# GpSimd's deviations in two sets, its semaphore clears behind them, at the start of four stages

## What is computed

```python
h = K(log_dt, inv_A_real, A_imag, B_ri, x)            # state-space kernel as tokens, (8, 256, 256)
h = concat([cls_tok, h], axis=1)                      # 257 rows for each batch
h = h + banded_attention(layernorm(h))                # softmax of banded scores, projection
h = h + experts(layernorm(h))                         # top 2 of 8 experts, silu(xW1) * xW3, then W2
h = h + fused_attention_block(layernorm(h))           # 16 heads + sparse top-k branch, x = LN(src + fused),
                                                      # LN(x + relu(x ff1) ff2)
h = h + fp4_ffn(layernorm(h))                         # block-wise FP4 rounding of activations and weights

def layernorm(x):
    return (x - mean(x)) / sqrt(var(x) + 1e-5)
```

## Time and profile before

| what | value |
| --- | --- |
| median of 3 runs | 1482.91 us (1480.83 to 1487.86) |
| the profiled execution, its own time | 1477.99 us |
| its span, first to last instruction | 1476.2 us |
| mean granted TensorE clock | 0.832 of full |
| TensorE matmul, busy | 1118.4 us (76%) |
| VectorE, busy | 765.7 us (52%) |
| GpSimd, busy | 452.8 us (31%) |
| ScalarE, busy | 384.5 us (26%) |
| starts of the four stages in the span | about 281, 603, 1135 and 1282 us |

### The profile page before, as it was taken

One profiled execution on the slowest core, in us unless ns is written; L12 is line 12 of the kernel. 1 busy time (PEld: TensorE's weight loads), 2 busy tenths in 40 slices (PEclk: granted clock), 3 DMA queues, 4 the chain that ended last, 5 costly groups with the idle time before them and its releaser, 6 DMA issues. The chain is left out here.

```text
span 1476.2 us, 21690 instructions
## 1 busy us (share of the span) xinstructions
PE 1118.4 (76%) x6799; PEld 807.9 (55%) x6799; DVE 765.7 (52%) x1788; ACT 384.5 (26%) x951; POOL 452.8 (31%) x527
## 2 busy tenths in 40 slices
PE   0358886750999990359999999999734999779888
PEld 0257774650677660235665665665422899646555
DVE  8955663230122224445556556656512377578885
ACT  0333331000222220114333334333210444222221
POOL 5941010117000007511202202211000577456665
PEclk9989998555899995667779769878657899989999
DMA  6016000102121113144314315414031200000000
GB/s 217 2 41 216 0 0 1 54 15 100 55 64 58 60 48 99 36 77 95 85 34 105 84 32 105 96 37 90 18 74 37 101 0 0 1 1 14 14 7 22
DMA packets 53403, 81.06 MB, mean 55 GB/s; under 512 B 8544, under 2 KB 45736, under 8 KB 52176
## 3 DMA queue, kind: packets, MB, share of 16 engines
q1 hardware_dynamic: 50128, 71.71, 19.1%
q0 software_dynamic: 3200, 8.43, 1.8%
HBM read 52.23 MB, written 27.62 MB: 54 GB/s over the span
## 5 line engine op out<-in xcount | busy, mean ns | idle before, releaser
L1933 DVE TENSOR_REDUCE fa_nm<-fa_ps 128x2 f32<-128x514 f32 x128 | 82.9, 690 | 74.4 <-PE fa_ps L2154 73.6
L1292 PE MATMUL ex_ps<-we_raw,ex_xT 128*128 x320 | 118.3, 494 | 0.0
L1773 ACT ACTIVATE fa_eT<-fa_ps 128x512 f32<-128x512 f32 x128 | 73.6, 590 | 81.7 <-PE fa_ps L2207 80.3
L1086 POOL DMA_INDIRECT ex_got<-y_rows,ex_pos_i x34 | 32.1, 943 | 196.9 <-DMA y_rows<-ex_y 186.8
L2945 PE MATMUL qf_ps<-qf_wg,qf_xT 128*128 128x352 f32 x272 | 89.9, 480 | 2.1 <-ACT qf_xT L2786 1.4
L2154 PE MATMUL fa_ps<-fa_ks,fa_qs 64*128 64x258 f32 x256 | 71.4, 408 | 15.4 <-DMA fa_ks<-fa_qk_rows 10.8
L447 PE MATMUL tk_ps<-tk_u,tk_qb 64*32 64x64 f32 x1024 | 22.8, 266 | 71.4 <-POOLq L314 59.7
L2207 PE MATMUL fa_ps<-fa_qs,fa_ks 66*128 66x256 f32 x256 | 71.3, 373 | 6.9 <-ACT fa_eT L1773 6.9
L1219 DVE COPY ex_hT<-ex_ps 128x384 f32<-128x384 f32 x40 | 22.3, 558 | 100.1 <-PE ex_ps L1301 100.1
L2154 PEld LDWEIGHTS fa_ps<-fa_ks,fa_qs 64*128 64x128 f32 x256 | 50.7, 258 | 40.6 <-issue 23.4
L2945 PEld LDWEIGHTS qf_ps<-qf_wg,qf_xT 128*128 128x128 f32 x272 | 50.6, 194 | 37.3 <-issue 6.6
(11 more groups left out here) (435 smaller groups left out, 2509.3 us busy)
## 6 DMA issues: line engine op xcount, KB each, us to landing
we_raw<-in_L_ffn_W SPq DMA_DIRECT2D x24, 384.0 KB
fa_qs<-fa_qk_rows SPq DMA_DIRECT2D x16, 514.0 KB
fa_ks<-fa_qk_rows SPq DMA_DIRECT2D x32, 257.0 KB, 9.9
x_rows<-tk_zero SPq DMA_DIRECT2D x1, 5120.0 KB, 19.1
ex_xin<-x_rows SPq DMA_DIRECT2D x40, 128.0 KB
y_rows<-ex_y SPq DMA_DIRECT2D x40, 128.0 KB, 1.7
fa_rsb<-fa_rs_rows SPq DMA_DIRECT2D x8, 528.0 KB
fa_qk_rows<-fa_qhl SPq DMA_DIRECT2D x32, 128.5 KB
```

Of the source, the lines that this page charges most:

```text
L1086: g.indirect_dma_start(out=got[0:n, a, t, :], out_offset=None, in_=y_rows[:, :], in_offset=bass.IndirectOffsetOnAxis(ap=pos_i[0:n, a, t:t ...
L1292: last = mm(ps[:, bank + t % 2, 0:HD], xT[:, t % 2, k, :], raw[:, ds(e, 1), m, k * HD:(k + 1) * HD], start=(k == 0), stop=(k == KC - 1))
L1773: cp(eT[:, j % 8, :], ps[:, ST + j % 2, :], ACT.Exp).then_inc(z["e_ready"], 1)
L1933: nc.vector.tensor_reduce(nm[:, :, j], ps[:, b:b + 2, 0:TOK], AX.X, ALU.max, negate=True).then_inc(z["max_done"], 1)
```

## The change

In the experts, the feed-forward and the quantised part, GpSimd makes the deviations (and where there is one, the shift) of tiles 0 and 1 first, increments `norm_ready`, makes those of the other 15 tiles, increments it again, and only then clears the old semaphores. In the experts VectorE waits for the second increment after it has normalised tiles 0 and 1. In the feed-forward and the quantised part ScalarE waits for it after it has centred tiles 0 and 1. In the fused attention, whose deviations were in two sets already, the clears move from the start to behind the scaling of `wf_o`, ahead of the second set. In the feed-forward SP issues the columns first, with a semaphore of their own (`columns_in`) for which ScalarE waits, then W1 and W2, then the five rows, then the raw weights; `own_in` now counts the five rows, and GpSimd and VectorE wait for these.

```diff
--- before.py
+++ after.py
@@ -1052,10 +1052,12 @@
 
         @block.gpsimd
         def _(pool):
+            s = Steps(pool, z["pst"])
+            reciprocal_deviation(nc, pool, mem, s, (slice(0, 2),))
+            pool.sem_inc(z["norm_ready"], 1)
+            reciprocal_deviation(nc, pool, mem, s, (slice(2, TILES),))
+            pool.sem_inc(z["norm_ready"], 1)
             clear_spent(pool, mem)
-            s = Steps(pool, z["pst"])
-            reciprocal_deviation(nc, pool, mem, s)
-            pool.sem_inc(z["norm_ready"], 1)
             g = nc.gpsimd
 
             s(g.memset(ones[:, :], 1.0))
@@ -1135,6 +1137,8 @@
             for u in range(BATCH):
                 normalise(nc, mem, 2 * u, xn[:, 2 * u, :])
                 normalise(nc, mem, 2 * u + 1, xn[:, 2 * u + 1, :]).then_inc(z["xn_ready"], 1)
+                if u == 0:
+                    dve.wait_ge(z["norm_ready"], 2)
             normalise(nc, mem, CLS, xn[:, CLS, :]).then_inc(z["xn_ready"], 1)
 
             dve.wait_ge(z["lg_ps"], BATCH + 1)
@@ -1578,7 +1582,6 @@
 
         @block.gpsimd
         def _(pool):
-            clear_spent(pool, mem)
             s = Steps(pool, z["pst"])
             g = nc.gpsimd
 
@@ -1595,6 +1598,7 @@
             pool.wait_ge(z["sig_ready"], 1)
             step(g.tensor_scalar(w["o"][:, :, :], w["o"][:, :, :], sg[:, 0:1], None, ALU.mult))
             pool.sem_inc(z["wo_ready"], 1)
+            clear_spent(pool, mem)
             reciprocal_deviation(nc, pool, mem, s, (slice(2, CLS),))
             shift(nc, pool, mem, s, (slice(2, CLS),))
             pool.sem_inc(z["norm_ready"], 1)
@@ -2382,7 +2386,7 @@
     XB, HB, YB = 0, 2, 6
 
     names = ("norm_ready", "xn_ready", "x_ps", "xt_ready", "xb_ready", "hid_ps", "hid_ready", "y_ps", "ag_ready",
-             "dev_ready", "hb_ready", "h_done", "vst", "pst", "y_read", "fetched", "own_in", "f1_in", "f2_in", "w_scaled", "w_rounded", "dve_go", "pool_go")
+             "dev_ready", "hb_ready", "h_done", "vst", "pst", "y_read", "fetched", "own_in", "columns_in", "f1_in", "f2_in", "w_scaled", "w_rounded", "dve_go", "pool_go")
     z = {n: sem("ff_" + n) for n in names}
 
     def tile_of(t, u):
@@ -2400,10 +2404,11 @@
     with nc.Block() as block:
         @block.sync
         def _(sp):
-            for dst, src in own:
-                sp.dma_start(dst, src).then_inc(z["own_in"], 16)
+            sp.dma_start(*own[-1]).then_inc(z["columns_in"], 16)
             for name, (dst, src) in zip(("f1_in", "f2_in"), weights):
                 sp.dma_start(dst, src).then_inc(z[name], 16)
+            for dst, src in own[:-1]:
+                sp.dma_start(dst, src).then_inc(z["own_in"], 16)
             for dst, src in loads:
                 sp.dma_start(dst, src).then_inc(z["fetched"], 16)
             if loads:
@@ -2411,12 +2416,13 @@
 
         @block.gpsimd
         def _(pool):
+            s = Steps(pool, z["pst"])
+            for some in (slice(0, 2), slice(2, TILES)):
+                reciprocal_deviation(nc, pool, mem, s, (some,))
+                shift(nc, pool, mem, s, (some,))
+                pool.sem_inc(z["norm_ready"], 1)
             clear_spent(pool, mem)
-            s = Steps(pool, z["pst"])
-            reciprocal_deviation(nc, pool, mem, s)
-            shift(nc, pool, mem, s)
-            pool.sem_inc(z["norm_ready"], 1)
-            pool.wait_ge(z["own_in"], 16 * len(own))
+            pool.wait_ge(z["own_in"], 16 * len(own) - 16)
             s(nc.gpsimd.tensor_tensor(w["c2"][:, :], w["c2"][:, :], w["b1"][:, :], ALU.add))
             s.wait()
 
@@ -2496,7 +2502,8 @@
             act.wait_ge(z["norm_ready"], 1)
             centred(0, 0)
             centred(1, 1)
-            act.wait_ge(z["own_in"], 16 * len(own))
+            act.wait_ge(z["norm_ready"], 2)
+            act.wait_ge(z["columns_in"], 16)
             turned(0, 0)
             turned(1, 1)
             hidden(0, 0)
@@ -2548,7 +2555,7 @@
                 sums(u, p)
                 if not first:
                     finish(u - 1, 1 - p)
-            dve.wait_ge(z["own_in"], 16 * len(own))
+            dve.wait_ge(z["own_in"], 16 * len(own) - 16)
             s.begin()
             pipelined(dve, TILES, body)
             s.base, s.n = s.before + 6 * TILES - 3 + SCALED * PARTS, 0
```

## The result

| | before | after |
| --- | --- | --- |
| median | 1485.38 us (1480.83 to 1489.14, 4 runs) | 1464.85 us (1462.55 to 1468.01, 4 runs) |
| ratio, 95% interval | | 0.9882 (0.9847 to 0.9916) |
| profiled execution, span | 1477.99, 1476.2 us | 1462.55, 1460.8 us |
| mean granted TensorE clock | 0.832 | 0.842 |

The changed kernel is 1.2% faster; forecast were 1469.6 us and a range of 1464 to 1477. Timed twice more against the kernel before it gave ratios of 0.9921 (0.9893 to 0.9949) and 0.9909 (0.9884 to 0.9933), 11.7 and 13.5 us of some 1483, less than the 20.5 us between the medians of the first comparison.

What follows compares the result with a forecast made beforehand. A serial chain at each stage start (clears, deviations, centring, turning) was taken to bound what the edit can give. Savings 3.0 + 3.4 + 5.95 + 1.0 = 13.35 us give a median of 1469.6 us, range 1464 to 1477.

Steps and rivals of the forecast that it cites:

- The price of a clear: At the four stage starts: GpSimd's late first instruction is its semaphore clears, 66 to 72 ns each, 71 ns used.
- D: Rival, stage starts: delays are entry costs and stay, so only the split acts; 1483.7 us; chance 0.03.
- Experts: Experts' start: first gate products at 287.3 instead of 290.28, saving 3.0 us, or 2.3 by the port rule.
- port rule: Experts: VectorE's two normalises hold the port pair GpSimd needs, so the second set starts up to 0.7 us later.
- Fused attention: Fused attention's start: 54 clears leave the head, 3.9 us, less 0.45 us, saves 3.4 us; bounds 2.9 to 3.9.
- the collision: Fused attention: GpSimd, free only at 618.8, starts the low parts late after VectorE's high parts; SP passes on 0.45 us.
- rival B: Fused attention's loop: its phase eats the gain, seven units of 55.5 us against 53.5 cost 14 us; 1483.6; chance 0.06.
- C: Rival, fused attention's loop: granted clock falls, 9.4 us per TensorE-bound unit, 1507.4 us at four; slower; chance 0.04.
- Feed-forward: Feed-forward's start: turned(0) 6.7 us earlier, less 0.75 us for late bias rows, saves 5.95 us; bounds nothing to 6.4.
- A: Rival, feed-forward: rows land late, near 1154, with the 2.2 MB; only 7.4 us saved, 1475.5 us; chance 0.07.
- the late end: Feed-forward: W1 landing as late as 1143.95 against a need at 1142.1, which would cost 1.8 us.
- Quantised part: Quantised part's start: ScalarE copies turned weights from 1288.6 instead of 1289.63, handed on to the first grid; saves 1.0 us.

Runs made afterwards that it cites:

- waits moved: Changed kernel with four tiles in the experts' first set, second waits later, attention and feed-forward clears later, rows ahead of W2: 1465.95 us, ratio 0.9898 to the kernel before.
- best parts: The kernel with later second waits, but the experts' set whole and TensorE's wait for W2 moved to its first read: 1465.72 us, ratio 0.9876 to the kernel before.

## Why the prediction was right, and where it was not

**The price of a clear** holds: 66 to 72 ns before, 71 to 77 where they are doubled. The step that carries the forecast is confirmed by moving the clears and by doubling them, and D is excluded.

**Experts.** Forecast 3.0, measured 3.20, 3.45 and 3.02 less against the first profile of before. The trace differs from the working in one place: the second increment comes at 4.73 after the start instead of 4.4. The second set's addition takes 0.43 us beside VectorE's two normalises (0.27 for 17 columns alone in the earlier trace rows). From the port rule of the Trainium skill (SBUF — State Buffer, Who interferes with whom) the prediction worked out a price of up to 0.7 us; here the addition shows 0.16 us more and the increment comes 0.3 later than worked out. In the feed-forward, where ScalarE and not VectorE works beside it, the same addition takes 0.27 us. That is compatible with the rule in kind, and the attention shows it again (the 0.61 us below); no run isolates the port.

**Fused attention**, the term that was mis-sized: for the collision the sum has 0.45 us, and it measures 1.2 (low part at 16.04 after the start, 14.87 with the clears late). The working took GpSimd to be free at 618.8, 15.4 after the start, which is where the third step of `fa_dm` ends in the kernel before; it ends at 15.96. Two things make up the difference. The second set starts at 11.09 instead of 10.9, behind clears and their wait of 4.36 us, where the earlier trace rows give 3.9 and 0.19. And its last step, L492, takes 0.61 us beside VectorE's high parts where it took 0.27 before:

```profile
617.68 0.27 POOL L492 TENSOR_SCALAR nmr<-nmr 128x14 f32<-128x14 f32 x1
...
618.60 0.21 POOL L1605 TENSOR_SCALAR_AFFINE_SELECT fa_dm<-fa_dm 128x32 f32<-128x32 f32 x1
```

Over all thirteen profiles this step takes 0.60 to 0.62 us in the seven in which VectorE's high parts run beside it, and 0.27 in the other six. The prediction priced such an overlap in the experts and not here.

The low part starts 2.8 us earlier than before (16.04 and 18.86 after the start), where the sum has 3.4. The gain at the head product is 2.07, 1.79 and 1.64 us in the three profiles, under the bound of 2.9 that was named, and 2.0 to 2.5 in the four others with this attention. What is lost on the way lies in the transfers: between SP's first strip of the keys' parts and the head product stand 20.8, 21.1 and 21.2 us. Before, it was 20.0 and 21.6 in the two profiles, so that remainder is within what executions differ by.

**The loop behind it** (rival B). The stretch from the head product on took 491.6, 491.9 and 491.0 us in the changed kernel, and 490.6 and 501.7 in the kernel before. The addition that closes a batch:

```profile
895.57 0.69 DVE L2000 TENSOR_TENSOR z<-z,fa_ps 128x512 f32 x1 [1.56 <-PE fa_ps L2276]
...
949.73 0.69 DVE L2000 TENSOR_TENSOR z<-z,fa_ps 128x512 f32<-128x512 f32 x1 [1.25 <-issue]
```

54.2 us here, where the earlier trace rows have 51.5. For the five units between the first and the sixth closing addition the length goes with the granted clock, over all thirteen profiles: 51.5 and 52.6 us at 0.87, 53.8 to 55.0 at 0.81, 55.3 to 56.8 at 0.78 and 0.79, 57.0 to 58.1 at 0.76, 59.8 and 60.0 at 0.74 (one at 0.82 took 55.6). The unit of 51.5 did not return, so B held in kind: the five units together took 274.75 us instead of 271.81. These 2.9 us are smaller than what two executions of one kernel differ by. With the clears late the stretch was 495.9, 497.1 and 496.7, so the 1.5 us gained at the head did not arrive; but it was 495.9 and 496.1 as well in two kernels whose attention was that of the change, and 491.8 and 494.9 in two more. Whether an earlier head product itself lengthens the loop stays open.

**C.** The first two stretches of 56 us after the head product:

```profile
638.16:694.16 56.00, 48.81 (x217) 29.89 (x217) 34.85 (x87) 17.10 (x41) 7.74 (x12) 0.74 0.32 68
694.16:750.16 56.00, 53.22 (x302) 34.69 (x302) 30.96 (x82) 19.48 (x46) 9.80 (x12) 0.77 0.35 74
```

0.74 and 0.77 against 0.68 and 0.80 in the earlier trace rows: the same clock in sum. C did not come.

**Feed-forward.** The numbers came as worked out: `turned(0)` 5.89 (5.9 forecast), `c2` 13.09 (13.0), third turn 16.28 (16.3), saved 5.96 (5.95). W1 landed 5.2 us after its issue. Two of these agree closer than the working deserves. The `c2` sum was to wait for the rows, which land at 13.0, behind clears that end at 12.7; in two of three profiles the clears ended at 13.09, behind rows that landed at 12.6 or 12.7. And the 0.75 us lost up to the third turn was to be the rows' alone, with TensorE due as much earlier as it started earlier. Its 64 products ahead of that turn, of which the line of before is this, took 8.95 us then and 9.30 with the change:

```profile
1148.83 8.95 PE L2578 MATMUL ff_ps<-ff_xT,wg_f 128*128 128x128 f32 x64 [0.56 <-ACT ff_xT L2478]
```

More of them ran at 1.2 GHz, since they started 6.67 us earlier and the clock rose 5.9 us earlier. So 0.35 of the 0.65 us that were lost are TensorE's own; they ended at 16.14, and the turn, held by `xb` and the centring, followed 0.14 later. That the two sizes came out alike is luck.

A did not come; the last row landed 12.7 us after the first issue, not with the 2.2 MB. By the Trainium skill's ring order (DMA: Bandwidth & Descriptors, Queues, rings and completion order) the prediction left the late end out, and it did not occur. Strict from load to load the order was not: in the kernel with the attention's clears late the first row, issued behind W2, landed at 8.85 and W2 at 9.36.

The split had no part in the gain, which the working had not seen: it credited `turned(0)` with the sum of both edits, though one set alone would have been there at the same time.

What the sum had right for a reason it did not give is the clock. From where the clock goes to 2.4 GHz in the feed-forward, TensorE waits for nothing but 2.8 us ahead of its last product, and in twelve of thirteen profiles, of nine kernels, the rest of the stage takes the same time:

| kernel | first hidden product | clock at 2.4 GHz | stage | stage less that |
| --- | --- | --- | --- | --- |
| before | 13.51, 13.51 | 16.8, 17.4 | 147.4, 147.6 | 130.6, 130.3 |
| after (three) | 6.84, 6.85, 6.85 | 10.9, 10.3, 11.0 | 141.4, 141.4, 142.0 | 130.6, 131.1, 131.0 |
| clears moved only | 10.04 | 13.8 | 144.1 | 130.4 |
| SP's order undone | 10.14 | 14.1 | 144.3 | 130.3 |
| no split, new order | 6.71 | 10.2 | 141.0 | 130.8 |
| waits moved | 5.58 | 10.8 | 141.1 | 130.3 |
| best parts | 5.49 | 11.1 | 142.2 | 131.1 |

The kernel with the attention's clears late (11.5 and 130.8) and that with the rows ahead of W2 (10.7 and 131.0) fit in; the one with doubled clears (24.9) is at 133.2, 3.0 of it in its last second product. Down to a first product at 6.7 the clock comes 3.3 to 4.6 us behind it; from 5.5 it comes 5.2 and 5.6 behind, and the last 1.3 us of earlier start are worth nothing.

**Quantised part.** Forecast 1.0; the first grid is 1.10 us earlier in all three profiles of the change, and that part was right. The other 2.8 us are clock: 1.7 in the last down product and 1.1 in the first hidden products. These took 7.47 us before and 6.33 after, but 7.73 and 7.80 in the two other profiles of the change: chance. Behind them the rest of the stage takes 169.1 us in ten profiles and 170.8 in three, and the difference is the last down product: 4.74 us in both profiles of before and with the waits moved (granted clock 0.64), 3.05 in all others (1.00). The kernel with doubled clears, whose weight copies start 1.6 us later than before, is among these others, so the 1.7 us do not follow from an earlier start; what brings them is not shown.

**The sum.** By the starts alone the change is worth 3.2 + 2.1 + 6.0 + 1.1 = 12.4 us, against 13.35 forecast; the errors are the 1.3 us of the attention and a few tenths the other way. The 11.7 and 13.5 us of the two repeats fit. The 15.4 us between the two profiles do not come from the edits alone: 1.3 of them lie ahead of the first edit and 2.8 in the clock of the quantised part, against 1.1 that the attention's loop took longer. The 20.5 us between the medians of the first comparison did not come again, and its 1464.85 us lies near the lower end of the range; the repeats' 1467.99 and 1468.01 are nearer to the forecast 1469.6.

## What to carry to other kernels

Count what a queue does before its first useful instruction, semaphore clears too: the view shows only a late first row, and one price for different counts tells what it is. Splitting work so that a part is ready sooner pays only if the wait for the rest stands behind work that uses the first part; here it stood ahead of it, and one set did as well. Where the wait was moved behind, the starts came earlier, but the clock and the wait for W2 took it back. Here an earlier start of a TensorE-bound stretch was worth what it moved the clock's rise by: read the clock in windows of a microsecond before counting the gain. And where an engine clears semaphores and waits for a transfer too, the bracket names the transfer, since the clears have no rows: set the idle time beside that of a run in which the transfer is early.

## What the hardware showed that was not expected

- The clock, after an idle stretch of TensorE, does not rise sooner for every earlier start. In the experts the ranking products took 5.26 us from 32.0 after the start and 7.29 from 29.9; both ended at 37.2 or 37.3.
- One kernel's attention loop took 490.55 and 501.69 us in two executions, with clocks of 0.78 to 0.87 in its five middle units in the one and of 0.74 to 0.81 in the other. A single profile can't weigh an edit of under 10 us there.
- Five row loads of 128 KB each took 7.1 to 9.0 us to land behind 2 MB of weights, and 1 MB of W1, with only the 2 KB of columns ahead of it, took 5.2.
- A GpSimd step on 128x14 elements took 0.61 us instead of 0.27 beside two VectorE instructions on 128x514, in each of the seven profiles in which they meet.
